# Differential attention: bringing the two softmaxes onto the same partitions by small transfers, and subtracting them ahead of a transpose of 288 columns

## What is computed

```python
scores = jnp.einsum('bhqd,bhkd->bhqk', q, k)                 # q, k: (b, 2 * H, s, 8), v: (b, H, s, 16)
probs = jax.nn.softmax(scores, axis=-1).reshape(b, H, 2, s, s)
w = probs[:, :, 0] - lam * probs[:, :, 1]
attn = jnp.einsum('bhqk,bhkd->bhqd', w, v)
rms = jax.lax.rsqrt(jnp.mean(attn * attn, axis=-1, keepdims=True) + EPS)
attn = attn * rms * subln_g * (1.0 - LAMBDA_INIT)
```

## Time and profile before

| | us |
|---|---|
| median of three runs | 5898.13 |
| profiled execution, its own time | 5898.7 |
| its span in the trace | 5896.9 |
| DVE busy | 5455.9 (93%) |
| PE busy | 5596.6 (95%) |
| ACT busy | 4959.1 (84%) |
| POOL busy | 2044.6 (35%) |

### The profile page before, as it was taken

The page is one execution under the profiler, slowest core; times in us unless marked ns, Lnnn a source line. Parts: engine busy times, 40 slices in busy tenths (PEclk is TensorE's granted clock), DMA queues, the critical chain, the costliest instruction groups (busy, mean ns, idle before and its releaser), DMA issues. The chain is left out here.

```text
span 5896.9 us, 167685 instructions
## 1 busy us (share of the span) xinstructions
PE 5596.6 (95%) x50896; PEld 1959.0 (33%) x50896; DVE 5455.9 (93%) x6142; ACT 4959.1 (84%) x9174; POOL 2044.6 (35%) x3526
## 2 busy tenths in 40 slices
PE   8989999999999999999999999999999999997776
PEld 5542333333333333333333332333233333335424
DVE  7879999999999999999999999999999999977716
ACT  6758999999999999999999999999999999983313
POOL 7972222232332222222333222222333232236406
PEclk9989999999999999999999999999999999998888
DMA  5662222222222222322222222222222222215587
GB/s 194 225 191 55 50 51 53 53 53 53 52 53 53 50 50 51 53 53 53 52 53 53 50 52 49 51 53 53 53 52 52 53 50 50 51 48 183 199 352 300
DMA packets 408166, 495.27 MB, mean 84 GB/s; under 512 B 132051, under 2 KB 265331, under 8 KB 395235
## 3 DMA queue, kind: packets, MB, share of 16 engines
q1 hardware_dynamic: 406499, 485.74, 33.3%
q10 hardware_dynamic: 1024, 0.53, 0.0%
HBM read 360.60 MB, written 123.21 MB: 82 GB/s over the span
## 5 line engine op out<-in xcount | busy, mean ns | idle before, releaser
L813 DVE TENSOR_REDUCE largest<-at_ps_m 128x1 f32<-128x1024 f32 x4080 | 4662.6, 1210 | 36.7 <-PE at_ps_m L925 31.3
L781 ACT ACTIVATE at_e<-at_ps_e 128x512 f32<-128x512 f32 x8192 | 4410.1, 598 | 338.3 <-PE at_ps_e L894 125.4
L911 PE MATMUL at_ps_o<-at_e,at_v 128*32 128x256 f32 (+1 forms) x30720 | 2685.2, 421 | 36.3 <-ACT at_e L781 24.7
L894 PE MATMUL at_ps_e<-w_first 51*128 51x512 bf16 x8192 | 2515.5, 382 | 7.7 <-issue 2.1
L925 PE MATMUL at_ps_m<-w_first 48*128 48x512 bf16 x8160 | 2473.1, 383 | 36.7 <-DVE largest L813 30.9
L911 PEld LDWEIGHTS at_ps_o<-at_e,at_v 128*32 128x32 f32 x30720 | 849.1, 149 | 1564.9 <-issue 819.9
L894 PEld LDWEIGHTS at_ps_e<-w_first 51*128 51x128 bf16 x8192 | 551.2, 93 | 1692.4 <-ACT at_e L781 1660.8
L698 POOL TENSOR_TENSOR at_negated<-at_zeros,at_largest_t 128x32 f32<-128x32 f32 x256 | 64.7, 253 | 2709.1 <-DVE at_largest_t L820 2709.0
L925 PEld LDWEIGHTS at_ps_m<-w_first 48*128 48x128 bf16 x8160 | 556.0, 93 | 148.1 <-DVE largest L813 143.6
L741 POOL TENSOR_TENSOR at_rms<-at_mean_eps,at_minus_half 128x16 f32<-128x16 f32 x128 | 372.5, 2911 | 10.1
L722 POOL TENSOR_TENSOR at_second<-at_crossed_t,at_neg_lam 128x256 f32<-128x256 f32 x128 | 78.5, 613 | 586.7 <-DVE at_crossed_t L825 586.7
(11 more groups left out here) (131 smaller groups left out, 2975.9 us busy)
## 6 DMA issues: line engine op xcount, KB each, us to landing
w_first<-k_parts SPq DMA_DIRECT2D x1536, 64.0 KB
w_first<-q_parts SPq DMA_DIRECT2D x256, 192.0 KB
w_first<-q_parts SPq DMA_DIRECT2D x256, 128.0 KB
w_first<-in_w SPq DMA_DIRECT2D x32, 1024.0 KB, 23.9
ex_w_second<-in_w SPq DMA_DIRECT2D x32, 1024.0 KB, 25.9
q_parts<-pr_parts SPq DMA_DIRECT2D x96, 256.0 KB, 2.5
k_parts<-pr_parts SPq DMA_DIRECT2D x96, 256.0 KB, 2.5
pr_x_in<-in_x SPq DMA_DIRECT2D x16, 1024.0 KB, 5.8
```

What stands on the lines that cost most here:

```text
L781: nc.scalar.activation(e[:, j % E_BUFS], ps_e[:, bank(u, j)], ACT.Exp, scale=SCALE).then_inc(exp_done, 1)
L813: nc.vector.reduce_max(largest[:, u % 2, j // SIDE, j % SIDE:j % SIDE + 1], ps_m[:, j % 2], AX.X).then_inc(max_done, 1)
L894: nc.tensor.matmul(ps_e[:, bank(u, j)], k_stack[rows, u, pair, c, kt * P:(kt + 1) * P], q_stack[rows, u, pair, c, half * HALF:(half + 1) * ...
L911: last = nc.tensor.matmul(ps_o[32 * tile:32 * tile + 32, columns], v[:, u, tile // 2, first:first + 2 * VD * TILES - kt:TILES], e[:, (QUAD ...
```

## The change

Quad n's product of `sums` now goes to a tile `crossed` of 512 columns (`products`). Its two softmaxes, each on 16 partitions of a tile of 32, are then copied by SP with 16 transfers per quad (`move_sides`): each takes 16 partitions x 256 columns of one softmax and one side (half of the columns) to `by_side`, where the two softmaxes of one head and column lie on the same partition, and the two sides on different ones. POOL scales and adds there (`join`, into `joined`, 256 columns, with the 32 of the totals behind them), and DVE transposes `joined`, 288 columns where there were 544. `finish` loses the two steps of the subtraction. On POOL the product now stands between the two splits instead of behind both.

```diff
-            crossed, crossed_t = sb("crossed", [P, HALF + BLK]), sb("crossed_t", [P, HALF + BLK])
+            crossed, by_side = sb("crossed", [P, HALF]), sb("by_side", [P, 2, HALF // 2])
+            joined, joined_t = sb("joined", [P, HALF // 2 + BLK]), sb("joined_t", [P, HALF // 2 + BLK])
...
+            SIDE_DMAS = 4 * QUAD
...
+                def move_sides(n):
+
+                    sp.wait_ge(crossed_done, 2 * n + 1 + 2)
+                    if not (isinstance(n, int) and n == 0):
+                        sp.sem_inc(passed, 1)
+                        sp.wait_ge(joined_done, n)
+                    for g in range(QUAD):
+                        for softmax in range(2):
+                            for side in range(2):
+                                sp.dma_start(by_side[32 * g + VD * side:32 * g + VD * (side + 1), softmax],
+                                             crossed[32 * g + VD * softmax:32 * g + VD * (softmax + 1),
+                                                     side * HALF // 2:(side + 1) * HALF // 2]).then_inc(sides_moved, 16)
...
                 def second_half(n, u, more, load):
                     move_totals(n, 1)
+                    move_sides(n)
                     if more:
                         load_rows(n + AHEAD, (u + AHEAD) % BUFS, 1)
...
-                def finish(n, base):
+                def products(n):
 
 
                     pool.wait_ge(sums_read, 2 * n + 2 + 1)
                     if not (isinstance(n, int) and n == 0):
+                        pool.wait_ge(sides_moved, 16 * SIDE_DMAS * n)
+                    nc.gpsimd.tensor_tensor(crossed[:], sums[:, 0], sums[:, 1], ALU.mult).then_inc(crossed_done, 1)
+
+                def join(n, base):
+
+                    pool.wait_ge(totals_moved, 16 * TOTAL_DMAS * (n + 1))
+                    if not (isinstance(n, int) and n == 0):
                         pool.wait_ge(sums_turned, n)
...
+                    nc.gpsimd.tensor_tensor(joined[:, HALF // 2:], totals[:, 0], totals[:, 1], ALU.mult).then_inc(crossed_done, 1)
+                    pool.wait_ge(sides_moved, 16 * SIDE_DMAS * (n + 1))
+                    nc.gpsimd.tensor_tensor(second[:], by_side[:, 1], neg_lam[:].to_broadcast([P, HALF // 2]), ALU.mult).then_inc(
+                        pool_step, 1)
+                    pool.wait_ge(pool_step, base + 1)
+                    nc.gpsimd.tensor_tensor(joined[:, 0:HALF // 2], by_side[:, 0], second[:], ALU.add).then_inc(joined_done, 1)
...
                 def turn(n, rows, base):
                     if rows:
-                        for c in range(2):
-                            split(2 * (n + AHEAD) + c, base)
-                            base = base + SPLIT_STEPS
+                        split(2 * (n + AHEAD), base)
+                    products(n)
+                    if rows:
+                        split(2 * (n + AHEAD) + 1, base + SPLIT_STEPS)
+                        base = base + 2 * SPLIT_STEPS
+                    join(n, base)
                     finish(n, base)
...
                 def turn_sums(n):
 
                     dve.wait_ge(crossed_done, 2 * (n + 1) + 2)
-                    nc.vector.transpose(crossed_t[:], crossed[:]).then_inc(sums_turned, 1)
+                    dve.sem_inc(passed, 1)
+                    dve.wait_ge(joined_done, n + 1)
+                    nc.vector.transpose(joined_t[:], joined[:]).then_inc(sums_turned, 1)
```

More of the change, by code:

```diff
@@ L560, in attend @@
             sums, totals = sb("sums", [P, 2, HALF]), sb("totals", [P, 2, BLK])
-            crossed, crossed_t = sb("crossed", [P, HALF + BLK]), sb("crossed_t", [P, HALF + BLK])
-            second, both = sb("second", [P, BLOCKS, VD]), sb("both", [P, BLOCKS])
-            attn_t = sb("attn_t", [P, BLOCKS // 2, 2, VD])
-            attn, square = sb("attn", [P, BLOCKS, VD]), sb("square", [P, BLOCKS, VD])
+            crossed, by_side = sb("crossed", [P, HALF]), sb("by_side", [P, 2, HALF // 2])
+            joined, joined_t = sb("joined", [P, HALF // 2 + BLK]), sb("joined_t", [P, HALF // 2 + BLK])
+            second, both = sb("second", [P, HALF // 2]), sb("both", [P, BLOCKS])
+            attn_t = sb("attn_t", [P, BLOCKS, VD])
+            square = sb("square", [P, BLOCKS, VD])
             mean_eps, rms = sb("mean_eps", [P, BLOCKS]), sb("rms", [P, BLOCKS])
@@ L585, in attend @@
             ONES = 6
-            SPLIT_STEPS, FINISH_STEPS = 4, 11
+            SPLIT_STEPS, FINISH_STEPS = 4, 10
             DVE_HEAD_PERIODS, TURN_SUMS, TURN_OUT = 12, 5, 11
@@ L589, in attend @@
             TOTAL_DMAS = 2 * QUAD
+            SIDE_DMAS = 4 * QUAD
+            sides_moved, joined_done = sem("sides_moved"), sem("joined_done")
             passed = sem("passed")
@@ L707, in split @@
                     nc.gpsimd.tensor_tensor(parts[:, 2], rest[:], parts[:, 1], ALU.subtract).then_inc(split_done, 1)
-                def finish(n, base):
+                def products(n):
                     pool.wait_ge(sums_read, 2 * n + 2 + 1)
                     if not (isinstance(n, int) and n == 0):
-                        pool.wait_ge(sums_turned, n)
-                    nc.gpsimd.tensor_tensor(crossed[:, 0:HALF], sums[:, 0], sums[:, 1], ALU.mult).then_inc(crossed_done, 1)
-                    pool.wait_ge(totals_moved, 16 * TOTAL_DMAS * (n + 1))
-                    nc.gpsimd.tensor_tensor(crossed[:, HALF:], totals[:, 0], totals[:, 1], ALU.mult).then_inc(crossed_done, 1)
-                    pool.wait_ge(sums_turned, n + 1)
[L720 to L726, removed]
@@ new lines, in finish @@
+                def finish(n, base):
+                    pool.wait_ge(sums_turned, n + 1)
+                    attn = joined_t[:, 0:HALF // 2].rearrange("p (b v) -> p b v", v=VD)
+                    s1_s2 = joined_t[:, HALF // 2:HALF // 2 + BLOCKS].rearrange("p (s b) -> p b s", s=2)
+                    nc.gpsimd.tensor_tensor(both[:].rearrange("p (b s) -> p b s", s=2), s1_s2, s1_s2, ALU.mult).then_inc(pool_step, 1)
+                    nc.gpsimd.tensor_tensor(square[:], attn, attn, ALU.mult).then_inc(pool_step, 1)
@@ L727, in finish @@
                     pool.wait_ge(pool_step, base + 2)
                     nc.gpsimd.tensor_tensor(both[:], both[:], sixteen_eps[:], ALU.mult).then_inc(pool_step, 1)
-                    pool.wait_ge(pool_step, base + 3)
-                    nc.gpsimd.tensor_tensor(square[:], attn[:], attn[:], ALU.mult).then_inc(pool_step, 1)
-                    step = 5
+                    step = 4
                     width = VD // 2
@@ L742, in finish @@
                     pool.wait_ge(pool_step, base + step + 2)
[L743 to L746, removed]
+                    nc.gpsimd.tensor_tensor(attn_t[:], attn, rms[:].unsqueeze(2).to_broadcast([P, BLOCKS, VD]),
                                             ALU.mult).then_inc(attn_done, 1)
@@ L829, in turn_out @@
                     dve.wait_ge(out_stored[u % 2], 16 * QUAD * ((n + 2 - u % 2) // 2))
-                    nc.vector.transpose(out[:, u % 2], attn_t[:].rearrange("p b s v -> p (b s v)")).then_inc(out_done, 1)
+                    nc.vector.transpose(out[:, u % 2], attn_t[:].rearrange("p b v -> p (b v)")).then_inc(out_done, 1)
                 def period(n, u, g, tries, rows=True, last_quad=True, this_quad=True):
```

## The result

| | before | after |
|---|---|---|
| median, us | 5896.6 (5893.12 to 5898.53, 4 runs) | 7173.1 (7171.43 to 7180.83, 4 runs) |
| profiled execution, its own time | 5898.7 | 7171.43 |
| its span in the trace | 5896.9 | 7169.6 |
| DVE busy | 93% | 77% |

The changed kernel takes **1.216 times as long** (ratio 1.2163, 95% interval 1.2149 to 1.2177): 1276 us more, where the prediction said 398. Over 126 quads that is 10.1 us each.

What follows compares the result with a forecast made beforehand. DVE was taken as the bound; a chain of 11.98 us against 8.6, less 0.27 for the shorter transpose, adds 3.11 us for 126 quads (392) plus 6 once: 5898.7 + 398 = 6297 us, range 6170 to 6700.

Steps and rivals of the forecast that it cites:

- The bound: Attention stage: DVE bounds the kernel, busy 994 of 1000 us, with nothing it does covered.
- the slot: From the end of ACT's second-half copy to DVE's transpose of the sums: 8.6 us, fixed by DVE's place in its stream.
- The chain's form: Copy's end to transpose: SP start 0.18, totals 2.54, sides 5.49, landing 2.2, POOL 1.57; sum 11.98 us per quad.
- the price of an issue: SP's 16 side transfers: 0.321 us each, spaced 0.366 us, so the last starts 5.49 us after the first.
- the landing: Last side transfer, from its issue until landed: 2.2 us, the median of the totals; 1.7 at least.
- dear issue: Rival on SP: each SBUF-to-SBUF transfer costs 0.589 us like the totals, wait 7.4 us per quad, 6807 us; chance 0.16.
- the pause: PE's standstill in DVE's wait: less than 4 us per quad, with PE keeping its full clock.
- the rival of 0.15: PE falls to its low clock in each wait: 2.6 us more per quad, 328 us, 6625 us; chance 0.15.
- The two rivals: Costlier SP issues, 898 + 10 us, chance 0.16; and PE's low clock in each wait, 328 us, chance 0.15.
- What is late next: SP's second-half score-row loads, behind the sides, start 4.5 us later but stay some 3 us ahead of PE; no added term.
- Hidden, faster: Rival: the side transfers fit before DVE's transpose, issues at most 0.14 us apart, DVE gains 34 us, 5865 us; chance 0.05.
- the estimate ahead: SP's issue by the skill page: 512 cycles at 1.2 GHz, 0.427 us; the time would be about 6500 us.

Runs made afterwards that it cites:

- runs 2 and 3: Changed kernel with the 16 side transfers going to DRAM, 6856.37 us; and with them moving 32 of 256 columns, 7164.1 us.
- run 6: Changed kernel with 8 of the 16 side transfers, POOL adding what lies in place by partition factors: 6440.62 us, ratio 1.0921.
- run 2: Changed kernel with the 16 side transfers writing to DRAM instead of SBUF, same source, rows and bytes: 6856.37 us, ratio 1.1627.
- Run 8: Changed kernel, still 16 transfers, with DVE's transpose of the sums in period 7 instead of 5: 6997.39 us, ratio 1.1865.
- runs 6 to 12: Changed kernel with 8 transfers (Run 8: 16), then later transposes and new SP queue orders: ratios 1.0921, 1.0686, 1.1865, 1.0466, 1.0432, 1.0106, 0.9977.
- run 11: The kernel of run 10 with the 18 stack loads split, 9 moved behind the store of the output: 5962.23 us, ratio 1.0106.
- run 4: Changed kernel with PE repeating attempt 12's matmuls 32 times in the wait, on the attempts' row group alone: 7282.31 us, ratio 1.2349.
- run 5: Changed kernel with PE repeating attempt 12's matmuls 64 times in the wait, alternating between two row groups: 6979.35 us, ratio 1.1834.
- run 10: Changed kernel with 8 transfers, the parts' stores issued ahead of them, and the transpose in period 8 instead of 5: 6156.9 us, ratio 1.0432.

## Why the prediction was wrong, step by step

- **The bound and the slot were right.** DVE was the bound, the transpose of 288 columns took 478 ns behind a wait and 468 without one (466 predicted), and the slot of 8.6 us decided: DVE waited for what went beyond it, put down to POOL's sum as foretold.
- **The chain's form was right.** With measured prices it is 0.18 + 2.54 + 15 x 0.66 (16 sides in 10.92 and 10.00 us, less the last one's 0.59) + 1.8 + 1.57 = 16.0 us; the trace shows 16.5 and 15.8.
- **The term that failed first: the price of an issue.** I took 0.321 us "since its shape is the same on both sides as here", from a transfer from SBUF to DRAM on another queue. The only row from SBUF to SBUF was that of the totals, 0.589 us, and the sides took 0.589. That makes 15 x (0.66 - 0.366) = 4.4 us more; the landing gave 0.4 back (1.8 for 2.2). The wait is 7.5 us and not 3.4, about 520 us in all. The forecast had named this as "dear issue", with a chance of 0.16. Shape was not enough as a likeness: of runs 2 and 3 the one that changed the destination moved the length and the one that changed the bytes did not.
- **The step that failed second: the pause was taken to be too short for the clock to fall.** The forecast let PE keep its full clock, against the rival of 0.15, because the pause is short, "less than 4 us per quad". That is wrong at the forecast's own length too: in run 6 PE stood still for 2.05 us and its clock fell to 0.50. So the low clock does not hang on the dear issue: no run had a wait of just 3.4 us, but it fell with DVE's wait at 2.3 us (run 6) and at 5.1 (run 2). It cost DVE 2.2 us of idle time per quad (2.6 in the rival), about 277 us.
- **The sum of the misses.** Per quad it is 4.1 us of wait, 2.2 of low clock and 0.5 of lone maxima, which no term had: 6.8 us, and 9.95 - 3.11 = 6.84 were missing. The two rivals' prices added, 898 + 10 + 328 us on 5899, give 7135 against 7173 measured. That is close in part by luck, since the clock cost 0.4 less than its rival had and the lone maxima made up for it.
- **The range** ended at 6700 us. It left out the dear issue even alone (6807 us), and no case had both.
- **"What is late next" was wrong in its reason, right in effect.** The rows did not delay PE in the changed kernel, but not because they were early: SP issued their load at 2037.58, 3.2 us after the sides and 16.9 us behind the copy, and PE was late too. Run 8 shortened the stall to 3.1 us, and PE waited for the rows, 7.5 us at most.
- **"Hidden, faster" has a counterpart** (the ratios of runs 6 to 12): the transpose's 34 us came within reach, of these runs, only when eight issues were saved, the slot was nearly twice as long, and three queue orders were changed. Then about half of them remain. Other ways were not tried.

## What to carry to other kernels

When no row has a transfer's source, destination and queue together with its shape, the price of its issue is open: take the dearest row that shares source and destination into the range, and multiply by the number of issues before choosing. Here that term was 4.1 of the 6.8 us per quad that were missing. A row of equal shape misled, and three kinds of transfer from SBUF to DRAM on one queue took 0.322, 0.420 and 0.639 us. When a step makes an engine wait, ask what else the wait sets off (the clock of a PE that stands still, here even for 2 us), and give the case in which two rivals hold together a price of its own before giving the range its end. When a stall is removed, look at what it covered: three times in a row the next late thing was another transfer on SP, and moving nine loads (run 11) was worth 195 us, where the shorter transpose is worth 34.

## What was not expected of the hardware

- An issue from SBUF to SBUF on SP took 0.589 us with 1 KB and with 128 bytes per row. To DRAM it took 0.420, and rows of 8 partitions from DRAM 0.278. "DMA: Bandwidth & Descriptors" of the Trainium skill, section "Why a DMA increments its semaphore by 16 and not by 1", gives one figure of 512 cycles, by the estimate ahead 0.427 us; the runs show issues from 0.278 to 0.639 us by kind, and of the lengths named here only the 0.420 us are near it.
- PE's clock fell while the profile shows PE busy without a gap, when only one group of 48 rows worked (run 4), and held with two groups in turn (run 5). Whether the rows or the denser pace (64 matmuls in 7.3 us against 30 in 9.4) made that difference was not told apart. It also fell when PE stood still for 2.05 us (run 6).
- Four stores took over 5 us to be usable with 18 loads ahead of them and the transfer engines busy for 0.54 of the time (run 10), and 1.0 us with 9 loads fewer ahead and a share of 0.02 (run 11).
